# Two attention layers over four images: the next image's first chunk moves between an image's layers

## The reference

```python
# layer 0: keys, queries of 32 rows; softmax over i, so each output column j sums over all 4096 i
q = Wq @ xf + bq;  k = Wk @ xf + bk;  v = Wv @ xf + bv
attn = softmax(q^T k, axis=1)
x = gamma * (v @ attn) + xf
# layer 1: keys and values are pooled 2x2, so there are 1024 of them
theta = conv(x);  phi = maxpool2(conv(x));  g = maxpool2(conv(x))      # 32, 32, 128 rows
attention = softmax(theta^T phi, axis=-1)
y = gamma1 * conv_out(g @ attention^T) + x
```

## Time and profile before

| what | us |
|---|---|
| median of three runs (lowest, highest) | 2719.68 (2712.09, 2726.18) |
| the profiled execution | 2717.54 |
| its span | 2715.7 |
| TensorE busy | 2610.4 |
| VectorE, GpSimd, ScalarE busy | 2036.5, 1979.4, 1741.6 |
| mean granted TensorE clock, share of full | 0.986 |

### The profile page before, as it was taken

How to read it: one execution, slowest core, us unless ns; L and a number is a source line. 1 busy time by engine, 2 the same in 40 slices (tenths; PEclk the granted TensorE clock), 3 DMA queues, 4 the chain that set the end, 5 groups by cost and what they waited for, 6 DMA issues and landing times.

```text
span 2715.7 us, 38345 instructions
## 1 busy us (share of the span) xinstructions
PE 2610.4 (96%) x11632; PEld 2078.7 (77%) x11632; DVE 2036.5 (75%) x3351; ACT 1741.6 (64%) x3171; POOL 1979.4 (73%) x1546
## 2 busy tenths in 40 slices
PE   7999999989999999998999999999899999999988
PEld 6788788777678888887678888888667888888765
DVE  7678777767777777776777777787677777877665
ACT  5566666667756666666775666666676666666566
POOL 3677777767867777775886777777588777777668
PEclk9999999999999999999999999999899999999989
DMA  2000000012110000001220000000121000000011
GB/s 90 1 16 16 17 24 17 24 40 71 63 32 21 20 23 18 17 16 41 70 78 24 17 24 16 17 16 17 47 79 63 16 16 16 17 17 16 17 47 63
DMA packets 45552, 85.28 MB, mean 31 GB/s; under 512 B 5032, under 2 KB 5160, under 8 KB 45352
## 3 DMA queue, kind: packets, MB, share of 16 engines
q1 hardware_dynamic: 37720, 68.41, 7.6%
q10 hardware_dynamic: 7632, 14.42, 1.8%
HBM read 49.03 MB, written 33.55 MB: 30 GB/s over the span
## 4 chain that ended last, share of the span: by engine, by line
PE 78%; DVE 12%; issue 5%; ACT 2%; POOL 1%; DMA 1%; SPq 0%; ACTq 0%; POOLq 0%; DVEq 0%
PE o_ps L914 16%; PE o_ps L917 16%; PE o_ps L918 16%; PE s_ps L891 9%; PE aux L954 8%; DVE mx L740 5%; DVE acc L702 3%; PE aux L928 2%; PE aux L992 1%; PE aux L975 1%; PE aux L932 1%; DVE aux L781 1%; PE aux L971 1%; POOL prob_l L502 1%; ACT queries L589 1%
## 5 line engine op out<-in xcount | busy, mean ns | idle before, releaser
L502 POOL TENSOR_TENSOR prob_l<-prob,prob_h 128x512 fp32r<-128x512 f32 x1280 | 1665.7, 1309 | 628.5 <-ACT prob_h L564 622.2
L561 ACT ACTIVATE prob<-s_ps 128x512 f32<-128x512 f32 x1280 | 766.8, 599 | 781.9 <-PE s_ps L891 779.8
L740 DVE TENSOR_REDUCE mx<-aux 128x1 f32<-128x512 f32 x1097 | 749.0, 683 | 290.9 <-PE aux L954 285.6
L914 PE MATMUL o_ps<-prob_h,vh 128*128 128x512 f32 x2304 | 912.4, 396 | 0.7
L917 PE MATMUL o_ps<-prob_l,vh 128*128 128x512 f32 x2304 | 903.6, 392 | 2.5 <-POOL prob_l L502 2.2
L918 PE MATMUL o_ps<-prob_h,vl 128*128 128x512 f32 x2304 | 900.8, 391 | 0.0
L702 DVE TENSOR_TENSOR acc<-prob,acc 128x512 f32<-128x512 f32 x1152 | 790.1, 686 | 61.9 <-ACT prob L561 49.6
L564 ACT ACTIVATE prob_h<-s_ps 128x512 fp32r<-128x512 f32 x1280 | 764.4, 597 | 0.0
L891 PE MATMUL s_ps<-queries,keys 128*128 128x512 f32 x1280 | 514.8, 403 | 22.9 <-DMA queries<-nm_turned 11.6
L914 PEld LDWEIGHTS o_ps<-prob_h,vh 128*128 128x128 f32 x2304 | 434.7, 189 | 101.2 <-ACT osb L575 9.8
L917 PEld LDWEIGHTS o_ps<-prob_l,vh 128*128 128x128 f32 x2304 | 434.4, 189 | 101.1 <-POOL prob_l L502 11.6
(11 more groups left out here) (131 smaller groups left out, 1845.4 us busy)
## 6 DMA issues: line engine op xcount, KB each, us to landing
xa<-x SPq DMA_DIRECT2D x32, 512.0 KB, 3.7
spill<-xa SPq DMA_DIRECT2D x32, 512.0 KB, 2.7
xa<-spill SPq DMA_DIRECT2D x32, 512.0 KB, 3.7
y<-xa SPq DMA_DIRECT2D x32, 512.0 KB, 2.8
xp<-x ACTq DMA_DIRECT2D x26, 512.0 KB, 3.7
queries<-nm_turned SPq DMA_DIRECT2D x236, 1.0 KB
xp<-x SPq DMA_DIRECT2D x2, 512.0 KB, 9.5
prob<-w_in ACTq DMA_DIRECT2D x1, 640.0 KB, 5.9
```

The source lines that it names most:

```text
L502: nc.gpsimd.tensor_tensor(out=prob_l[:, i, :], in0=prob[:, i, :], in1=prob_h[:, i, :].bitcast(f32), op=ALU.subtract).then_inc(pl_ready, 1)
L561: nc.scalar.activation(prob[:, i, :], s_ps[s][:, :], ACT.Exp).then_inc(p_ready, 1)
L740: ins = nc.vector.tensor_reduce(out=dst, in_=bank[:, :], axis=AX.X, op=ALU.max)
L914: mm(o_ps[ct][:, :], value(vh, l, t, ct), prob_h[:, i, :], start=t == 0, stop=False)
```

## The change

The list of chunks is now written out (`sequence`): the first chunk of image b+1 stands between layer 0 and layer 1 of image b. No gate is left but the last image's (`GATE`). For this the next image's keys and values are made during the last chunk of layer 0, by tables that name a step, a place and a bank (X0 or X1) for every job; the keys go into a ring of 9 chunks, the values over those that the running chunk has attended. The values of chunks 6 and 7 are made in the moved chunk, for which chunk 6 of x is rounded a second time. 16 STs of layer 1 go to the ends of chunks 5 and 6, 8 into the last chunk, 16 into the moved one. All rows of maxima now go by DMA. Chunks 6 and the moved one are no longer wide (22 wide chunks, not 28). To make room, `prob` and `prob_l` have 3 slots, `xa` has 3, and x's loads are all issued by SyncE.

```diff
-RING = 4
+RING, PRING = 4, 3
-QSLOTS = 12
-ASLOTS, PSLOTS = 4, 2
+QSLOTS, KSLOTS = 16, KC[0] + 1
+ASLOTS, PSLOTS = 3, 2
+def sequence():
+    order = [(0, 0, n) for n in range(NCH)]
+    for b in range(B - 1):
+        order.append((0, b + 1, 0))
+        order += [(1, b, n) for n in range(NCH)]
+        order += [(0, b + 1, n) for n in range(1, NCH)]
+    return order + [(1, B - 1, n) for n in range(NCH)]
 def wide(l, b, n):
-    return l == 0 and n < NCH - 1
+    return l == 0 and n < (NCH - 2 if b + 1 < B else NCH - 1) and not (n == 0 and b > 0)
 def begin_step(h, ahead):
-    return max(h - ahead, tile_no(l, b, 0) if gated(l, b) else 0)
+    return max(h - ahead, GATE if h >= GATE else 0)
+ROUNDS0 = ((2, (10, 1), (10, 3), (11, 1)), (3, (12, 1), (12, 3), (13, 1)), (4, (14, 3), (15, 1), (15, 3)),
+           (5, (18, 1), (18, 3), (19, 1)), (6, (22, 1), (22, 3), (23, 1)), (7, (24, 1), (24, 3), (25, 1)))
+KEYS0 = ((0, (1, 1), X1, (2, 1)), (1, (2, 3), X1, (3, 3)), (2, (11, 3), X1, (12, 3)), (3, (15, 1), X1, (16, 1)),
...
+        elif more:
+            for c, at, *low_at in ROUNDS0:
+                put(g + at[0], at[1], Job("X", 0, b + 1, c, 0))
+                for k in range(CT):
+                    put(g + low_at[k][0], low_at[k][1], Job("XL", 0, b + 1, c, k))
+            second_layer(g, *prev[1:], (5, 1), ((5, 3), (6, 3)), (7, 1), (8, 1), (8, 3), (9, 3, X0), (11, 1, X0), (11, 3))
+            for c, _, _, low_at in KEYS0:
+                put(g + low_at[0], low_at[1], Job("K0L", 0, b + 1, c, 0))
+            values0(g, b + 1, VALUES0)
+            for c, at, where, _ in KEYS0:
+                put(g + at[0], at[1], on(Job("K0", 0, b + 1, c, 0), where))
+            place_maxima(g, of(1, b, 4, 0) + of(1, b, 5, 0), MAXIMA1)
+            for c in range(KC[0]):
+                place_maxima(g, of(0, b + 1, 0, c), MAXIMA0[c])
+            put(g + 27, 3, Job("M", 0, b + 1, 0, 0))
+            put(g + 29, 3, Job("X", 2, b + 1, NCH - 2, 0))
...
-        if more:
-            k0, k0l, v00, v00l, v01, v01l = project0(b + 1, 0, (S1, Y, S0))
-            k1_, k1_l, v10, v10l, v11, v11l = project0(b + 1, 1, (S2, X1, S1))
...
+        def key_chunk(b, c):
+            return chunk((c - b) % KSLOTS)
...
             def split_prob(h):
-                i = h % RING
+                i = h % PRING
                 pool.wait_ge(ph_ready, h + 1)
-                wait(pool, av_done, h - RING + 1)
+                wait(pool, av_done, h - PRING + 1)
...
             def exps(h):
-                wait(act, pl_ready, h - RING + 1)
-                wait(act, acc_done, h - RING + 1)
+                wait(act, pl_ready, h - PRING + 1)
+                wait(act, acc_done, h - PRING + 1)
...
                     if l == 0:
-                        biased(0, keys[0][KQ_K, chunk(c)], bank[KQ_K, :], KQ_K)
+                        if b and c:
+                            act.wait_ge(s_full, tile_no(0, b - 1, NCH - 1, SUBS * c - 1) + 1)
+                        biased(0, keys[0][KQ_K, key_chunk(b, c)], bank[KQ_K, :], KQ_K)
...
                     at = c * SUBS + 2 * k
+                    if b:
+                        act.wait_ge(av_done, tile_no(0, b - 1, NCH - 1, at + 1) + 1)
```

More of the change, by code:

```diff
@@ L76, in chunk_before, with own_x1 @@
-    return (k // NCH % 2, k // (2 * NCH), k % NCH) if k >= 0 else None
+    i = POSITION[l, b, n]
+    return SEQ[i - 1] if i else None
 def wide(l, b, n):
-    return l == 0 and n < NCH - 1
-def gated(l, b):
-    return l == 1 or b == 0
+    return l == 0 and n < (NCH - 2 if b + 1 < B else NCH - 1) and not (n == 0 and b > 0)
+WIDE_NO = {chunk: i for i, chunk in enumerate(c for c in SEQ if wide(*c))}
+SECOND_BEFORE = {chunk: sum(c[0] for c in SEQ[:i]) for i, chunk in enumerate(SEQ)}
+def own_x1(b, c):
+    return not (c == 0 and b > 0)
@@ new lines, in second_layer_from, with values0, place_maxima @@
+    def second_layer_from(h, b, c):
+        second_layer(h, b, c, (5, 1), ((6, 1), (8, 1)), (10, 1), (11, 1), (12, 1), (13, 3, X1), (15, 1, X1), (16, 1))
+    def values0(g, b, table):
+        for c, k, _, _, low_at in table:
+            put(g + low_at[0], low_at[1], Job("V0L", 0, b, c, k))
+        for c, k, at, where, _ in table:
+            put(g + at[0], at[1], on(Job("V0", 0, b, c, k), where))
+    def place_maxima(g, jobs, slots):
+        for (l, b, n, kc, s), (t, place, at) in zip(jobs, slots, strict=True):
+            put(g + t, place, maxima(l, b, n, kc, s, at))
@@ new lines, in make_plan @@
+    b, c = B - 1, NCH - 1
+    last = (0, b, c)
+    d2 = on(Job("D2", *last, 0), X0)
+    k1, g1 = on(Job("K1", 1, b, c, 0), X0), on(Job("G1", 1, b, c, 0), S0)
+    t1 = on(Job("T1", 1, b, c, 0), S0)
+    st = [maxima(1, b, 0, 1, s, (X1, Y, S1, S2)[s]) for s in range(SUBS)]
+    add = [Job("N", *last, k) for k in range(CT)]
+    rnd = rounding(1, b, c)
+    k1k, k1q, k1m, k1l = (Job(name, 1, b, c, 0) for name in ("K1K", "K1Q", "K1M", "K1L"))
+    t1l = Job("T1L", 1, b, c, 0)
+    before[GATE] = [d2, *add, *rnd, k1, k1k, g1, k1m, t1, *st, Job("M", 1, b, 0, 0), k1q, k1l, t1l]
@@ L185, in make_plan @@
[L185 to L193, removed]
@@ L215, in make_plan @@
                     put(g, 1, Job("M", 1, b, n + 1, 0))
-                if n in (4, 5):
+                if n in (4, 5) and not more:
                     for i in range(2):
                         put(g + 5 + i, 1, maxima(1, b, NCH - 1, 0, 2 * (n - 4) + i, X1))
+            elif more:
+                first = (0, b + 1, 0)
+                put(g, 1, on(Job("D2", *first, 0), X0))
+                for k in range(CT):
+                    put(g + 1 + k, 1, Job("N", *first, k))
+                put(g + 1, 1, Job("M", 0, b + 1, 1, 0))
             else:
@@ L298 @@
         LAST_ON_Y[_job.b + 1 if _job.l else _job.b] = _job
+X_BEFORE = [max((q for q in range(r) if X_SLOT[q] == X_SLOT[r]), default=None) for r in range(len(X_SLOT))]
 for _g, _jobs in BEFORE.items():
```

397 lines of the change are left out of this document (204 added, 193 removed).

## The result

The changed kernel takes 2823.33 us (median; 2819.52 to 2830.58) against 2721.3 for the kernel before in the same comparison: a ratio of 1.0382, 95% interval 1.0346 to 1.0418. It is slower by 3.8%. Forecast were 2739 us and a range up to 2764, so the sign was right and the size far off.

The account below looks back on a forecast made before the run. TensorE was taken to bound the kernel, GpSimd layer 1 alone. A turn sums to 297.2 us against 292.6, 13.8 more for three; 5.2 for two rows of maxima gives 2736.5 profiled, 2739 us median, range 2695 to 2764.

Parts of the forecast that it names:

- the last chunk of layer 0: Last chunk of layer 0 in each turn: 92.8 us of work plus waits, 115.8 us in all.
- my stretches: Five groups of steps in layer 0's last chunk, losing 4.4, 6.7, 2.0, 7.4 and 2.2 us to waits.
- 22 and the ordinary 1.0: Layer 0's last chunk: 22 us of bank and queue waits, plus the 1.0 us an ordinary chunk loses.
- the banks cost, the queues don't: Rival on layer 0's last chunk: 7 us of queue waits absorbed, 15 left, no change at 2718 us; chance 0.2.
- They become like the last image's: 8 x 12.7 = 101.6 us: Layer 1 of each turn: eight chunks at the last image's GpSimd-bound pace, 101.6 us.
- it touches little else: Outside the turns between images the change would alter little; an ordinary chunk of layer 0 stays at 62.6 us.
- the 5.9 us a turn: Edits elsewhere: 16 more STs ending chunks 5 and 6 (3.6 us), chunk 6's small matmuls and Z in chunk 1 (2.3 us).
- the moved chunk: Next image's first chunk, placed before layer 1: 72.2 us of work plus small losses, 73.9 us.
- 1.7 us for all of these: Waits in the moved chunk: the ordinary 1.0 us plus 0.7 us for two rows of maxima on VectorE.
- The clock or the ring: Rival: low clock in layer 0's last chunk, or three slots slowing layer 1; much slower, 2761 us; chance 0.12.
- over 13.3: Sign in layer 1: more than 13.3 us a chunk would show the three-slot ring was mis-sized.
- the row at 1286 us: Old profile's layer 1 chunk at clock 0.92, 1.5 us longer, read as slow clock after TensorE stood at the gate.

Follow-up runs that it names:

- the last experiment's kernel: Changed kernel with sums begun by a copy, old list of steps, earlier roundings of chunks 6 and 7, and 16 STs of the moved chunk left out: 2719.5 us.
- the copy: Changed kernel with a chunk's sums begun by copying tile 0's exponentials into acc, so no sum reads two SBUF operands: 2782.34 us.

## Why the prediction was right or wrong

*Right: the last chunk of layer 0.* Lost over the work in image 1's last chunk, by my stretches (steps 0 to 7, 8 to 17, 18 to 21, 22 to 25, 26 to 28): 5.0, 7.4, 2.3, 7.2 and 3.2 us for 4.4, 6.7, 2.0, 7.4 and 2.2. That is 25.1 us for 22 and the ordinary 1.0. The 9.1 us that image 2 lost in steps 8 to 17 had 3.4 us of low clock in them. The waits for `xl` ahead of K0 of chunks 6 and 7 were 1.6 and 0.7 us, where I had named 1 to 3. Two of the waits as TensorE's timeline of image 1 in the last experiment's kernel has them, the second half of `xl` in K1 (1.7 forecast for the rounding there), and V0 of chunk 2 behind K0L (2.0 forecast):

```profile
1209.43 0.50 PE L1028 MATMUL aux<-xl,wh 128*128 128x512 f32 x1 [1.27 <-POOL xl L625]
...
1231.90 0.39 PE L1081 MATMUL aux<-wh,xh 128*128 128x256 f32 x1 [2.16 <-DVE mx L848]
```

The runs above show that both kinds of wait are real, so the rival "the banks cost, the queues don't" fell too: earlier roundings alone gave 14 us back.

*Wrong, the largest part: the step "They become like the last image's: 8 x 12.7 = 101.6 us".* It took 107.8 to 117.1. The term 8 x 12.7 held GpSimd's own pace, and this was right: without the long sums layer 1 takes 99.5 to 101 us. What it lacked is what an unbroken GpSimd can do to VectorE, and through VectorE to D2 and the exponentials. Such a stream was in the last image's layer 1 before, with a first sum of 1.87 us in it, and I read the chunks there and not VectorE's records. 35.5 us of the miss. The Trainium skill has the rule: "GPSIMD Engine Reference", section "1. Specifications", lists SBUF interfaces shared with VectorE and contention with VectorE's instructions that have two SBUF inputs. The trace agrees, at 4.3 to 5.65 us for a sum of 0.69; I hadn't weighed it. The Trainium skill's "SBUF — State Buffer", section "SBUF: two separate sides", says that whoever starts first holds the port pair for its whole instruction. By that a sum waits for one GpSimd instruction, 1.3 us, and ends within 2 us of its start, as all did before; the trace of after shows waits over four or five instructions in a row, which that rule alone doesn't give.

*Wrong: "it touches little else".* I costed the 16 added STs and the chunk that is no longer wide, 5.9 us a turn, and passed over the moved steps 3, 6, 18 and 25 of the list for all the other chunks, taking an ordinary chunk as unchanged. The 24 chunks numbered 1 to 6 took 29.2 us more than forecast, and with the old list 27.8 of them went; the 5.9 us a turn were right, 6.4 with the old list. The working was at hand: K0L's hold on a bank stood in my own account of the last chunk, and by the plan the new ST at step 18 is the next use of X1 behind K1.

*Wrong in size: the moved chunk*, 3.8 us each. TensorE's waits in that of image 1's turn, in the changed kernel:

```profile
PE aux L1062 <- DVE nm_cols L861: 1.2, 1, 1.2
PE aux L1083 <- DVE vl L828: 0.8, 2, 0.4
PE aux L1049 <- DVE nm_cols L861: 0.6, 2, 0.3
PE aux L1049 <- DVE queries L829: 0.5, 1, 0.5
PE aux L1026 <- DVE mx L850: 0.2, 1, 0.2
```

I had 1.7 us for all of these, and they are 3.3: D2 and ST behind the rows of maxima on VectorE, ST behind the subtraction of K1, V0 behind the subtraction of the V0 before it. Of the other 2.2 us most belong to the same seven waits: from start to start of the matmuls they cost 4.3 us, not 3.2, and the matmul behind each comes another 0.1 us late. No run tested this term.

*The rivals.* "The clock or the ring" gave 13.6 us a chunk of layer 1 as what the ring would bring, and over 13.3 was to show it; 14.2 came, so this sign pointed at a cause that the runs don't bear out: the ring alone did nothing in the kernel before, and the copy took the loss away with the ring of three in place. The last chunk of layer 0 had a clock of 1.00, 1.00 and 0.99. The clock fell in layer 1, to 0.93, 0.95 and 0.91 in the mean. It fell within seven of the eight stops ahead of D2, and 0.3 us behind the end of the eighth; so the low clock there followed the long sums, though 3.4 us of it in image 1 and in image 2 came without one. With the copy layer 1 had 1.00, 1.00 and 0.98. My reading of the row at 1286 us was wrong in one point: the low stretch in it began at 1300.1, 24 us behind the one at the gate.

*Open:* why VectorE gets in between two instructions in one chunk and only behind the row in another. In the last image a first sum started just ahead of a row of splits both before (0.05 us) and after (0.03); it lasted 1.87 us before and 4.31 after.

## What to carry to other kernels

Before a stretch is made denser on GpSimd, look in it for VectorE's instructions with two SBUF operands and give them one from PSUM; a copy ahead cost nothing here where the engine had room (2718.72 us for the kernel before with it). When a change rewrites a table of steps, cost the row that repeats 25 times before the one that repeats three times. Where two waits end close together, remove both before judging either, and read the granted clock of the stretch in every version.

## What was not expected of the hardware

- A VectorE sum of two 128x512 fp32 operands from SBUF (0.69 us) took 4.3 to 5.65 us beside GpSimd splits without a pause, eight times in 64; a copy with one SBUF operand at the same place never took over 0.70, and the sum never over 1.28 where the splits were 0.73 to 0.90 us long with pauses.
- A VectorE sum that got in between two GpSimd instructions made one of them last 1.71 to 1.75 us instead of 1.3 and took 1.36 to 1.87 us itself; one that didn't ended 0.56 us behind the last instruction of GpSimd's row.
- Within seven of the eight stops of TensorE of 2.9 to 3.8 us ahead of D2, and 0.3 us behind the eighth, the granted clock fell to its low level, for 6.8 us seven times and 3.4 once. In a chunk of layer 1 with one such stop of 3.58 us it was 0.90 in the mean; with the copy, without stops, it was 1.00 through the whole of layer 1 of the same image.
